# Attention tiles with 64 columns of their own for each half of 64 tokens (320 columns for 384), without block mask rows, and reciprocals spread as two 16-bit halves

## The chip, the cores and the metric

The kernel runs on one core of a Trainium2 chip. The metric is the time of the whole program on the device, in microseconds. Everything below is about that one core: its TensorE (PE; PEld is its weight load), VectorE (DVE), ScalarE (ACT), GpSimd (POOL), and SyncE (SP), whose queue issues most of the DMAs.

## The reference, cut to what matters

Two layers work on x of 8 sequences x 1024 tokens x 256. Each is an attention of 16 heads with 16 dimensions a head, and a feed-forward part; the change touches the attentions and the step that follows the first one.

```python
# layer 0: every query sees the keys at most 128 tokens away
out_of_window = abs(idx[:, None] - idx[None, :]) > 128
att = softmax(where(out_of_window, fmin, q @ k.T) / 16)
x = x + (att @ v) @ Wp.T + bp
# then a mixture of 8 experts, on layernorm(x)
# layer 1: blocks of 64 tokens; block 0 and the last block see all keys, a middle
# block n sees block 0, blocks n-1, n, n+1 and the last block (blocks 1 and -2 alike)
ctx = softmax(q @ k.T * 0.25 over those keys) @ v
x = x + ctx
# then a ternary linear layer, on x
```

## The kernel before, in words

`stage_attend` (lines 453 to 883) is built twice, as "a0" for layer 0 and "a1" for layer 1. Its unit of work is one sequence and one group of four heads: 32 units a layer. Tokens are cut in 8 tiles of 128. A list of jobs says which keys a tile of queries is multiplied with. In layer 0 (`window_jobs`) tile t takes the columns of tiles t-1, t and t+1: 384 columns, 256 for the first and the last tile, so 6 jobs of 384 and 2 of 256. In layer 1 (`block_jobs`) tile 0 holds the first and the last block and takes all 1024 columns in two jobs of 512; tiles 7 to 1 take tile 0 and their neighbourhood with half a tile on each side: 384 columns, 320 for tiles 7 and 1. That is 9 jobs. Blocks that only one half of a tile may see are taken out by four more rows in the contraction (`block_rows`, loaded by ACT's queue in `start`, lines 760 and 761), so that the product of -65504 and 32768 is added there.

Each job of each of the four heads is done twice on TensorE, both times by `product` (line 769, the matmul is line 775):

- `score_tile` makes scores with the queries' tile as the stationary operand, into a bank of the ring psc (3 banks). DVE's `maxima` takes the maximum of each row: in layer 0 with a mask added (line 687, a custom instruction followed by a read of its accumulator), in layer 1 with a plain reduction (line 692). POOL scales the maxima, TensorE turns them (line 809), ACT copies them (line 718), and SP's queue stores them as one more row of the operand (`rows_of_max`, line 582).
- `prob_tile` makes the same scores with the keys' tile as the stationary operand and the maximum subtracted, into a bank of pst (3 banks). ACT takes the exponential (line 740) into pr. In layer 0 POOL sets the corners outside of the window to zero (line 658). `with_v` multiplies by the values (line 836): 17 columns stationary for each of four heads at the tile positions 0, 32, 64 and 96, in 32-bit, which the compiler makes two passes of one matmul.

The contraction has 48 to 53 rows, so heads go in pairs, one on rows 0 to 63 of the array and one on rows 64 to 127. The order of the work is written out by hand in TensorE's `step`: for each job two blocks of (probabilities n, scores n of the unit after next, probabilities n+1, scores n+1), and behind each block half of the `with_v` of an earlier job (two jobs before in layer 0, one in layer 1). The first two units' scores are made alone, in `start`. In the last two units no scores are left to make.

SP's queue carries, for each unit: 12 loads of q and k (lines 564 and 565, `reload_qk`, after the last `prob_tile` of the unit before), 4 stores of maxima (line 582, `rows_of_max`), the load of the values (line 574), 4 stores of the output (line 598) and one of the sums (line 600), in that order.

`stage_combine` ("c0") divides the output of layer 0 by its sums and multiplies by Wp. `Shares` makes the reciprocals (`invert`, DVE line 905) and spreads a head's reciprocal over its 16 rows by a matmul with a 0/1 matrix (`over_rows`, line 912), in 32-bit: two passes of 512 columns for each of two halves e and each of 16 chunks c. DVE multiplies (line 1022), ACT and POOL split the product in two 16-bit halves (992, 1007), TensorE multiplies by Wp (lines 68 to 70, 24 matmuls of 256 columns a chunk), DVE adds (1029) and takes statistics (112).

## Time and profile before

| | |
|---|---|
| Median of 3 runs | 2443.06 us (2439.72 to 2443.52) |
| The profiled execution's own time | 2437.45 us |
| Its span from the first to the last instruction | 2435.7 us |
| Busy share of the span | PE 90%, DVE 76%, ACT 68%, POOL 44% |
| Attention of layer 0 | about 165 to 695 us |
| Combination | about 700 to 790 us |
| Attention of layer 1 | about 1671 to 2300 us |

In the rows below a group of instructions is named by its line, its engine and "out<-in" with the program's names for tiles, and by its shape: 48*128 48x384 is a matmul of 48 contracted rows, 128 stationary columns and 384 moving columns. A timeline row gives the start, the time from the first start to the last end, how many instructions it merges (x4), and in brackets how long the engine was idle before and what ended that. A matmul's length in the trace contains the latency of the array, so the distance from start to start says what it costs when many follow each other. SPq is SyncE's queue, each row the issue of a DMA.

### The profile page before, as it was taken

The page shows a single profiled execution, that of the slowest core. Times are in us where ns is not written, and L with a number is a line of the kernel's source. Part 1 is how long each engine was busy: PE and PEld are TensorE (multiplying, and loading weights), DVE is VectorE, ACT ScalarE, POOL GpSimd, SP SyncE. Part 2 cuts the span into 40 slices and gives each one's busy share as a digit, 9 for nine tenths or more (in the row PEclk, how much of TensorE's full clock was granted, in tenths as well). Part 3 has the DMA queues.
Part 4 walks back from the last instruction along what each step waited for, and adds up shares of the span by engine and source line. Part 5 has one row for each costly group of instructions (what it writes and reads, how often), then busy time and mean ns, then how long its engine had stood idle before and what let it go on. Part 6 is the DMA issues. An engine that isn't in the chain of part 4 may idle for free. (4 is left out here: it accounts for less than half of the span.)

```text
span 2435.7 us, 73430 instructions
## 1 busy us (share of the span) xinstructions
PE 2200.0 (90%) x25549; PEld 1344.8 (55%) x25549; DVE 1840.5 (76%) x5599; ACT 1661.7 (68%) x3892; POOL 1072.9 (44%) x1370
## 2 busy tenths in 40 slices
PE   7979999999969688879999995996999999999765
PEld 4643444444436576768888884563444444444354
DVE  5539999999829577755445444984999999999298
ACT  7955888889942555525445443893699999999644
POOL 3533666666654466646666664562000000000076
PEclk9987999999979899989999998997899999999888
DMA  6552333333232567646654344884232232322242
GB/s 231 199 183 72 91 91 92 92 90 92 67 89 77 138 189 187 163 129 125 144 127 106 92 92 118 270 274 149 63 80 74 78 79 78 79 75 68 65 152 96
DMA packets 363698, 289.65 MB, mean 119 GB/s; under 512 B 228401, under 2 KB 296753, under 8 KB 363345
## 3 DMA queue, kind: packets, MB, share of 16 engines
q1 hardware_dynamic: 349616, 248.24, 37.2%
q0 software_dynamic: 12960, 35.60, 4.5%
q8 instruction: 220, 3.60, 0.6%
q10 hardware_dynamic: 768, 1.12, 0.2%
q14 instruction: 134, 1.09, 0.1%
HBM read 133.53 MB, written 123.69 MB: 106 GB/s over the span
## 5 line engine op out<-in xcount | busy, mean ns | idle before, releaser
L740 ACT ACTIVATE a_pr<-a_pst 128x384 f32<-128x384 f32 (+3 forms) x2176 | 908.8, 486 | 117.0 <-PE a_pst L775 79.7
L775 PE MATMUL a_psc<-a_ke,a_qe 52*128 52x128 f16 (+5 forms) x3072 | 648.6, 291 | 32.7 <-DMA a_ke<-mrow 29.2
L692 DVE TENSOR_REDUCE a_mx<-a_psc 128x1 f32<-128x384 f32 (+2 forms) x1152 | 566.9, 564 | 18.9 <-PE a_psc L775 13.7
L775 PE MATMUL a_pst<-a_qe,a_ke 53*128 53x128 f16 (+5 forms) x3072 | 564.3, 281 | 2.7 <-ACT a_pr L740 0.4
L836 PE MATMUL a_po<-a_pr,a_ve 128*17 128x128 f32 (+3 forms) x10496 | 562.1, 302 | 2.0 <-ACT a_pr L740 1.2
L687 DVE CUSTOM_DVE_ANT_0 a_cut<-a_psc,row_mask 128x384 bf16<-128x384 f32 (+1 forms) x1024 | 472.7, 521 | 23.4 <-PE a_psc L775 11.5
L775 PEld LDWEIGHTS a_pst<-a_qe,a_ke 53*128 53x128 f16 (+1 forms) x3072 | 210.3, 94 | 330.1 <-ACT a_pr L740 187.5
L658 POOL TENSOR_SCALAR_AFFINE_SELECT a_pr<-a_pr 128x512 f32<-128x512 f32 x448 | 275.1, 634 | 163.2 <-ACT a_pr L740 163.2
L775 PEld LDWEIGHTS a_psc<-a_ke,a_qe 52*128 52x128 f16 (+1 forms) x3072 | 223.5, 94 | 143.7 <-DVE a_mx L692 44.5
L836 PEld LDWEIGHTS a_po<-a_pr,a_ve 128*17 128x17 f32 x10496 | 193.9, 96 | 191.2 <-issue 116.3
L638 POOL TENSOR_SCALAR a_mneg<-a_mx 128x32 f16<-128x32 f32 x64 | 18.4, 288 | 632.5 <-DVE a_mx L696 588.1
L1671 DVE SCALAR_TENSOR_TENSOR e_hid<-e_pgu,e_gate 128x256 f32<-128x256 f32 x213 | 90.5, 425 | 213.0 <-ACT e_gate L1615 211.9
L68 PE MATMUL e_pgu<-e_xt,uh 128*128 128x256 f16 x852 | 233.3, 274 | 8.1 <-DMA e_xt<-xs 8.1
L315 POOL TENSOR_TENSOR p_stg<-p_qk,p_stg 128x512 f16<-128x512 f32 x128 | 164.4, 1290 | 159.7 <-ACT p_qk L355 157.2
L70 PE MATMUL e_pgu<-e_xt,ul 128*128 128x256 f16 x852 | 233.3, 274 | 0.0
L69 PE MATMUL e_pgu<-e_xt,uh 128*128 128x256 f16 x852 | 233.3, 274 | 0.0
L1615 ACT ACTIVATE e_gate<-e_pgu 128x256 f32<-128x256 f32 x213 | 81.5, 383 | 210.3 <-PE e_pgu L70 210.3
L1590 POOL TENSOR_TENSOR e_hl<-e_hid,e_hh 128x256 f16<-128x256 f32 x213 | 140.9, 675 | 121.1 <-ACT e_hh L1619 119.3
L1216 POOL DMA_INDIRECT xs<-g_xrow,g_slot x128 | 134.5, 1051 | 92.4 <-DVE g_slot L1348 60.2
L1598 POOL DMA_INDIRECT y<-e_yst,e_dest x142 | 138.0, 972 | 39.8 <-issue 23.4
L68 PE MATMUL e_py<-dh,e_hh 128*128 x426 | 116.2, 273 | 2.4 <-POOL e_hl L1590 2.4
L70 PE MATMUL e_py<-dh,e_hl 128*128 x426 | 116.2, 273 | 0.0
(234 smaller groups left out, 4172.7 us busy)
## 6 DMA issues: line engine op xcount, KB each, us to landing
a_qe<-qx SPq DMA_DIRECT2D x378, 64.0 KB, 2.6
a_ke<-kx SPq DMA_DIRECT2D x378, 64.0 KB, 2.7
vx<-p_vst SPq DMA_DIRECT2D x32, 544.0 KB, 3.4
a_ve<-vx SPq DMA_DIRECT2D x64, 272.0 KB, 3.1
qx<-p_stg SPq DMA_DIRECT2D x64, 256.0 KB, 3.4
kx<-p_stg SPq DMA_DIRECT2D x64, 256.0 KB, 3.3
ox<-a_ost SPq DMA_DIRECT2D x256, 64.0 KB
x_res<-x SPq DMA_DIRECT2D x16, 512.0 KB, 8.9
```

The costliest lines, as they stand in the source:

```text
L68: pe.matmul(out, stat_hi(p), mov_hi(p), start=(a == 0), stop=False)
L69: pe.matmul(out, stat_hi(p), mov_lo(p), start=False, stop=False)
L70: last = pe.matmul(out, stat_lo(p), mov_hi(p), start=False, stop=(a == n - 1))
L315: pool.tensor_tensor(stg[:, b % 2, m, 1, cols], qk32[:, m, :], stg[:, b % 2, m, 0, cols], ALU.subtract).then_inc(qk_lo, 1)
L658: pool.affine_select(out=edge, in_=edge, compare_op=ALU.is_ge, fill=0.0, base=0, pattern=[[0, 4], [sign, width]], channel_multiplier=-sign)\
L687: dve.tensor_tensor_reduce(out=cut[:, n % 4, 0:width], in0=psc[(u * n_s + n) % RING][:, 0:width], in1=row_mask[:, at:at + width], scale=1. ...
L692: dve.tensor_reduce(out.unsqueeze(1), psc[(u * n_s + n) % RING][:, 0:width], AXX, ALU.max)\
L740: act.activation(pr[s % SLOTS][:, h // 2, h % 2, 0:width], pst[prob_slot(u, n) % RING][:, 0:width], ACT.Exp, scale=scale).then_inc(p_ready, 1)
L775: last = pe.matmul(out[:, col:col + count], stat, mov(tok, count), start=(k == 0), stop=(k == len(pieces) - 1), skip_group_check=True, til ...
L836: last = pe.matmul(po[h][32 * a:32 * a + VW, tok % CH:tok % CH + w], ve[g][:, t, a * VW:(a + 1) * VW], pr[s % SLOTS][:, a // 2, a % 2, col ...
L1590: pool.tensor_tensor(hl[:, j % 2, f, :], hid[:, f, :], hh[:, j % 2, f, :], ALU.subtract)\
L1598: pool.indirect_dma_start(y2[:, :], bass.IndirectOffsetOnAxis(ap=dest[:, g, t:t + 1], axis=0), yst[:, g, t, :], None).then_inc(scattered[g ...
```

## The change

- Layer 0: a middle tile t takes one piece of 256 columns that both halves of its 128 tokens share (from 64 tokens before the tile to 64 behind it), and an edge of 64 columns in which each half has tokens of its own: the 64 before the piece for the first half, the 64 behind it for the second. 320 columns for 384. The first and the last tile keep 256.
- Layer 1: tiles 7 to 1 take tile 0 and their own tile as one strided piece of 256, and an edge of 64 for each half: 320 columns for all. The two jobs of 512 stay.
- `product` issues everything by halves of 64 stationary columns, at column position 0 or 64 of the array: two edge matmuls of 64 columns where a job has edges, two matmuls of 256 (or 512) columns, and in layer 0's `prob_tile` two more of 64 columns, which add a corner mask (`corner16`) to the edge. A score tile is 4 matmuls, a probability tile 6 in layer 0 and 4 in layer 1, where it was 1 in layer 0, 2 or 1 in layer 1; tiles without edges are 2.
- `with_v` multiplies the edge columns twice, once for each half's destination, with values whose other half of 64 rows is zero (`vez`). They are loaded by two more DMAs a unit on SP's queue, and the zeros are set once by POOL.
- Layer 0's POOL masks keep their number and are 64 wide for 128 in middle tiles; the mask of `maxima` comes from a loaded table `corner`.
- The four mask rows and their loads go (16 DMAs of ACT's queue in layer 1). Layer 0 loads `corner` by one DMA on ACT's queue.
- `Shares` splits the reciprocals in two 16-bit halves, the high one by ACT and the low one by DVE, each once for 512 columns and twice in the stage, and spreads them by two 16-bit matmuls.

```diff
+    jobs = [(0, [(0, 2 * P, 0)], None, [(P, P, 1, 0)])]
+    for t in range(1, TB - 1):
+        lo = t * P - 64
+        jobs.append((t, [(lo, 2 * P, 0)], (lo - 64, lo + 2 * P, True, True), [(0, 64, 0, 64), (3 * 64, 64, 1, 0)]))
+    return jobs + [(TB - 1, [(N - 2 * P, 2 * P, 0)], None, [(0, P, 0, 0)])]
...
+        left, right = t > 1, t < TB - 1
+        edges = (t * P - 64 if left else t * P, t * P + P if right else t * P + 64, left, right)
+        jobs.append((t, [(0, P, 0), (t * P, P, P)], edges, []))
...
+                v = vx[bass.ds(b * N, N), g * 4 * VW:(g + 1) * 4 * VW].rearrange("(t p) w -> p t w", p=P)
+                sp.dma_start(ve[g][:, :, :], v).then_inc(v_loaded[g], 16)
+                for half in range(2):
+                    r = slice(64 * half, 64 * half + 64)
+                    sp.dma_start(vez[r, half, g, :, :], v[r, :, :]).then_inc(v_loaded[g], 16)
...
+                pool.memset(vez[64:P, 0, :, :, :], 0.0).then_inc(vez_set, 1)
+                pool.memset(vez[0:64, 1, :, :, :], 0.0).then_inc(vez_set, 1)
+                pool.wait_ge(vez_set, 2)
...
+            if jobs[s][2]:
+                a, b, left, right = jobs[s][2]
+                edges = [(1, a, 64, widths[s] - 64)] * left + [(2, b, 64, widths[s] - 64)] * right
...
-                    for col, width, which in jobs[s][2]:
+                    for col, width, which, base in jobs[s][3]:
...
-            def product(par, out, stat, mov, pieces, ready):
-
-                for k, (tok, count, col) in enumerate(pieces):
-                    last = pe.matmul(out[:, col:col + count], stat, mov(tok, count), start=(k == 0),
-                                     stop=(k == len(pieces) - 1), skip_group_check=True, tile_position=(64 * par, 0))
+            def product(par, out, t, stat, mov, job, cornered, ready):
+
+
+                _t, pieces, edges, _m = job
+                end = sum(p[1] for p in pieces)
+                halves = [slice(64 * half, 64 * half + 64) for half in range(2)]
+                for half in range(2) if edges else ():
+                    pe.matmul(out[halves[half], end:end + 64], stat[:, t * P + 64 * half:t * P + 64 * half + 64],
+                              mov[:, edges[half]:edges[half] + 64], start=True, stop=False, skip_group_check=True,
+                              tile_position=(64 * par, 64 * half))
+                for half in range(2) if edges and cornered else ():
+                    r = slice(64 * par, 64 * par + 64)
+                    pe.matmul(out[halves[half], end:end + 64], corner16[r, 0:64], corner16[r, 64 + 64 * half:128 + 64 * half],
+                              start=False, stop=False, skip_group_check=True, tile_position=(64 * par, 64 * half))
+                for half in range(2):
+                    if len(pieces) == 2:
+                        to = out[halves[half], 0:end].rearrange("p (t c) -> p t c", c=P)
+                        of = mov.rearrange("k (t c) -> k t c", c=P)[:, 0:t + 1:t, :]
+                    else:
+                        to, of = out[halves[half], 0:end], mov[:, pieces[0][0]:pieces[0][0] + end]
+                    last = pe.matmul(to, stat[:, t * P + 64 * half:t * P + 64 * half + 64], of, start=not edges, stop=True,
+                                     skip_group_check=True, tile_position=(64 * par, 64 * half))
                 last.then_inc(ready, 1)
...
+                            cols = slice(a * VW, (a + 1) * VW)
+                            stat = vez[:, kind - 1, g, t, cols] if kind else ve[g][:, t, cols]
                             last = pe.matmul(po[h][32 * a:32 * a + VW, tok % CH:tok % CH + w],
-                                             ve[g][:, t, a * VW:(a + 1) * VW], pr[s % SLOTS][:, a // 2, a % 2, col:col + w],
+                                             stat, pr[s % SLOTS][:, a // 2, a % 2, col:col + w],
...
+    def high(self, act, half):
+        cols = slice(half * CH, half * CH + CH)
+        act.wait_ge(self.ready, half + 1)
+        act.activation(self.rec_hi[:, cols], self.rec[:, cols], ACT.Copy, scale=SHS).then_inc(self.high_done, 1)
+
+    def low(self, dve, half):
+        cols = slice(half * CH, half * CH + CH)
+        dve.wait_ge(self.high_done, half + 1)
+        dve.scalar_tensor_tensor(out=self.rec_lo[:, cols], in0=self.rec[:, cols], scalar=SHS, in1=self.rec_hi[:, cols],
+                                 op0=ALU.mult, op1=ALU.subtract).then_inc(self.low_done, 1)
+
     def over_rows(self, pe, out, c, e):
         if c < 2:
             pe.wait_ge(self.set, 3)
-            pe.wait_ge(self.ready, c + 1)
+            pe.wait_ge(self.low_done, c + 1)
         at = ((c // 2) * EC + e) * P
-        return pe.matmul(out, self.spread[:, at:at + P], self.rec[:, (c % 2) * CH:(c % 2) * CH + CH],
-                         start=True, stop=True)
+        cols = slice((c % 2) * CH, (c % 2) * CH + CH)
+        pe.matmul(out, self.spread[:, at:at + P], self.rec_hi[:, cols], start=True, stop=False)
+        return pe.matmul(out, self.spread[:, at:at + P], self.rec_lo[:, cols], start=False, stop=True)
```

## Rows read from the trace of the kernel before

**Rows 1.** Busy time by engine in 60 us of each attention (windows)
```profile
300.00:360.00 60.00, 59.72 (x829) 24.74 (x827) 58.58 (x255) 54.05 (x139) 40.00 (x68) 1.00 0.36 92
...
1800.00:1860.00 60.00, 60.00 (x1069) 29.87 (x1069) 59.38 (x125) 55.54 (x131) 0.86 (x3) 1.00 0.27 75
```

**Rows 2.** ACT's copy of the turned maxima, once a unit (timeline, both attentions)
```profile
409.08 0.25 ACT L718 ACTIVATE a_mt<-a_pst 32x128 f16<-32x128 f16 x1
...
424.27 0.26 ACT L718 ACTIVATE a_mt<-a_pst 32x128 f16<-32x128 f16 x1
...
1996.65 0.27 ACT L718 ACTIVATE a_mt<-a_pst 32x128 f16<-32x128 f16 x1
...
2014.69 0.27 ACT L718 ACTIVATE a_mt<-a_pst 32x128 f16<-32x128 f16 x1
```

**Rows 3.** DVE's maxima, three of layer 0 and a whole unit of layer 1 (timeline)
```profile
403.29 0.55 DVE L687 CUSTOM_DVE_ANT_0 a_cut<-a_psc,row_mask 128x384 bf16<-128x384 f32 x1
...
403.76 0.42 DVE L687 CUSTOM_DVE_ANT_0 a_cut<-a_psc,row_mask 128x256 bf16<-128x256 f32 x1
...
404.11 0.42 DVE L687 CUSTOM_DVE_ANT_0 a_cut<-a_psc,row_mask 128x256 bf16<-128x256 f32 x1
...
1682.98 17.35 DVE L692 TENSOR_REDUCE a_mx<-a_psc 128x1 f32<-128x512 f32 x36 [10.10 <-PE a_psc L775]
```

**Rows 4.** PE, blocks of products and of with_v, one after the other (timeline, both layers)
```profile
400.17 0.33 PE L775 MATMUL a_pst<-a_qe,a_ke 49*128 49x384 f16 x1
...
400.61 0.41 PE L836 MATMUL a_po<-a_pr,a_ve 128*17 128x128 f32 x8
400.95 0.33 PE L775 MATMUL a_pst<-a_qe,a_ke 49*128 49x384 f16 x1
...
401.65 0.63 PE L836 MATMUL a_po<-a_pr,a_ve 128*17 128x128 f32 x16
...
2001.12 0.23 PE L775 MATMUL a_pst<-a_qe,a_ke 53*128 53x128 f16 x1
...
2001.18 0.27 PE L775 MATMUL a_pst<-a_qe,a_ke 53*128 53x256 f16 x1
...
2001.56 0.41 PE L836 MATMUL a_po<-a_pr,a_ve 128*17 128x128 f32 x8
```

**Rows 5.** PE, 16-column products with 128 stationary columns, cold and warm clock (timeline)
```profile
2307.20 0.60 PE L1807 MATMUL t_ps<-ident,t_sums 16*128 16x16 f32 x4 [8.65 <-DMA t_ot<-ox]
2307.73 1.97 PE L1814 MATMUL t_pt<-ident,t_ot 128*128 128x128 f32 x8
...
2350.31 0.41 PE L1807 MATMUL t_ps<-ident,t_sums 16*128 16x16 f32 x4
2350.66 1.09 PE L1814 MATMUL t_pt<-ident,t_ot 128*128 128x128 f32 x8
```

**Rows 6.** SP's queue, one unit of layer 0 (timeline); its longest wait, 240 to 660 us
```profile
404.58 0.61 SPq L564 DMA_DIRECT2D a_qe<-qx  x1
...
413.27 2.78 SPq L582 DMA_DIRECT2D a_qe<-a_mt  x4
416.09 0.44 SPq L574 DMA_DIRECT2D a_ve<-vx  x1
416.64 3.25 SPq L598 DMA_DIRECT2D ox<-a_ost  x4
...
420.53 0.62 SPq L564 DMA_DIRECT2D a_qe<-qx  x1
...
SPq L564 <- PE a_pst L775: 20.0, 21, 1.9
```

**Rows 7.** The combination, one chunk on PE; DVE's waits, 728 to 780 us
```profile
725.71 1.88 PE L912 MATMUL c_pb<-c_rec,c_spread 128*128 128x512 f32 x4
...
730.05 1.88 PE L912 MATMUL c_pb<-c_rec,c_spread 128*128 128x512 f32 x4
...
DVE x_res L1029 <- PE c_py L70: 5.1, 12, 0.4
```

**Rows 8.** Layer 1's start: ACT's queue and PE's first product (timeline)
```profile
1676.04 0.71 ACTq L760 DMA_DIRECT2D a_qe<-brows  x1
...
1682.36 1.01 PE L775 MATMUL a_psc<-a_ke,a_qe 52*128 52x512 f16 x3 [15.69 <-DMA a_ke<-mrow]
```

More of the change, by code:

```diff
@@ L462, in stage_attend @@
     masked = row_mask is not None
-    KS = TK + (0 if const_rows is None else 4)
+    KS = TK
     KR = KS + 1
@@ L504, in stage_attend @@
         N_STORE = 5
-        N_CUT = sum(len(m) for _, _, m in jobs)
-        cuts_to = [sum(len(m) for _, _, m in jobs[:s + 1]) for s in range(nj)]
+        N_CUT = sum(len(job[3]) for job in jobs)
+        cuts_to = [sum(len(job[3]) for job in jobs[:s + 1]) for s in range(nj)]
+        widths = [sum(p[1] for p in job[1]) + (64 if job[2] else 0) for job in jobs]
         block = ctx.enter_context(nc.Block())
@@ L678, in maxima @@
                     j, par, i = n // 4, 1 - n % 2, n // 2 % 2
-                    t, pieces, mask_list = jobs[j]
-                    width = sum(p[1] for p in pieces)
+                    t, _p, edges, mask_list = jobs[j]
+                    width = widths[j]
                     out = mx2[:, u % 2, par, i, at_zero.index(j)] if len(at_zero) == 2 and t == 0 else mx[g % 2][:, par, i, t]
@@ L683, in maxima @@
                     if mask_list:
-                        at = 0 if t > 0 else P
+                        mask = corner[:, 0:width] if edges else row_mask[:, 0:width] if t else row_mask[:, P:P + width]
                         after(dve, s_read, u * n_s + n - 3)
@@ L731, in step @@
                 for s in range(nj):
-                    t, pieces, _m = jobs[s]
-                    width = sum(p[1] for p in pieces)
+                    width = widths[s]
                     after(act, p_used, u * nj + s - SLOTS + 1)
@@ L795, in prob_tile @@
                 s, i = n // 4, n // 2 % 2
-                t, pieces, _m = jobs[s]
                 if n == 0:
+                    if masked and unit(g, b) == 0:
+                        pe.wait_ge(c_rounded, 1)
                     pe.wait_ge(m_loaded[g], b * 64 + 64)
@@ L800, in prob_tile @@
                 free_to(pe, k - RING)
-                product(par, pst[k % RING], ke[g][rows(par, KR), i, t * P:(t + 1) * P],
-                        lambda tok, count: qe[g][rows(par, KR), i, tok:tok + count], pieces, t_ready)
+                product(par, pst[k % RING], jobs[s][0], ke[g][rows(par, KR), i, :], qe[g][rows(par, KR), i, :],
+                        jobs[s], masked, t_ready)
             def turn(g, b):
@@ L992, in high @@
                     act.activation(ah[:, c % AR, e, :], att[:, c % 2, e, :], ACT.Copy).then_inc(a_hi, 1)
+            for half in range(2):
+                shares.high(act, half)
             act.wait_ge(s_w, 16)
@@ L2034, in build @@
 def build(nc, x, l0_wqkv, l0_bqk, l0_bv, l0_wp, l0_bp, gate_w, up_w, down_w, l1_wqkv, l1_bqk, l1_bv,
[L2035 removed]
+          tern_w, tern_alpha, tern_bias, masks, out):
     qx = nc.dram_tensor("qx", [2, 2 * HG, DH, 2, T], F16, kind="Internal").ap()
```

118 lines of the change are left out of this document (61 added, 57 removed).

## The prediction

> **What bounds the kernel now.** I read the windows first, to see which engines are full in each attention, then the period of a unit, then what each engine needs of it if nothing holds it up. In both attentions PE and DVE are busy over 97% of 60 us, ACT about 90% [rows 1]. A full PE proves little, since its lengths hold latency, so I count from start to start. A unit lasts 424.27 - 409.08 = 15.19 us in layer 0 and 18.04 in layer 1 [rows 2]; some 30 of each 32 run at that pace.
>
> DVE: in layer 0 a maximum over 384 columns costs 0.47 and one over 256 costs 0.35 [rows 3], so 24 x 0.47 + 8 x 0.35 = 14.1 us of 15.19. In layer 1, while nothing else runs, the 36 of a unit take 17.35 [rows 3], about 17.5 with the join, of 18.04. DVE is the bound in layer 1, and in layer 0's wide jobs.
>
> PE: a block of four products of 384 columns takes 0.44 from its start to `with_v` (400.17 to 400.61), in layer 1 the same (2001.12 to 2001.56). `with_v` with 8 matmuls of 128 columns takes 0.34 and 8 more cost 0.22 (0.63 less 0.41) [rows 4]: 0.12 a block and 0.22 for 128 columns. 256 columns stream in 0.11 less 384's 0.16, so a block of 256 is 0.33. Layer 0: 12 x 0.44 + 4 x 0.33 = 6.6, `with_v` 22 x 0.22 + 16 x 0.12 = 6.8 (2816 columns a unit), 0.15 for the turn: 13.5 of 15.19. Layer 1: 14 x 0.44 + 4 x 0.55 = 8.4, with_v 28 x 0.22 + 18 x 0.12 = 8.3, turn: 16.8 of 18.04. So PE stands 1 to 2 us behind DVE: it is next in line.
>
> SP's queue: its loop, from one unit's first load to the next one's, took 15.95 in the unit shown, with 8.69 for the 12 loads, 2.82 for the maxima, 0.55 for the values and 3.89 for the stores; it waits for PE 20.0 us in the 27.6 units of that stretch, 0.7 a unit [rows 6]. So it needs about 14.4 of layer 0's 15.19. In layer 1 it has over 3 us to spare.
>
> **The change, part by part.**
>
> DVE and ACT lose 64 columns in 24 tiles of layer 0 and in 20 of layer 1. At 0.12 for 128 columns [rows 3] that is 0.06 each: DVE needs 24 x 0.41 + 8 x 0.35 = 12.6 in layer 0 and 17.5 - 1.2 = 16.3 in layer 1. ACT, at most 54.05/60 of the period now, loses about as much. POOL is 67% busy in layer 0 and its masks get narrower. None of them bounds then.
>
> `with_v`: a middle job had 384 columns, and has 256 + 2 x 64 = 384: PE gains nothing there. It issues more pieces (240 matmuls a unit for 144 in layer 0); I take 0.1 a unit for them.
>
> Products: this decides. A block had 4 matmuls; it has 20 in layer 0's middle (6 + 4, twice) and 16 in layer 1. No row shows 64 x 64 tiles, so I bound a block from both sides. Low: all four quadrants of the array run beside each other and the longest chain counts, 64 + 64 + 256 in layer 0, as long as before (0.44), and 320 in layer 1 (0.44 less 2 x 0.03 = 0.38). That `with_v` runs its four column positions side by side, from separate data (8 matmuls, 0.34 in all), speaks for that [rows 4]. High: weight loads follow each other. Four 128-column loads with 16-column products take 0.35 warm and 0.53 cold [rows 5], so 64 columns cost at most 0.044 warm: 20 x 0.044 + 0.1 = 0.98, and 16 x 0.044 + 0.1 = 0.80. Between: matmuls start in the order of issue, so the second head's long matmul waits until the first one's has started, at 0.06 + 0.04 us, and the next pair needs its rows: 0.2 for one pair, 0.3 to the last long start, 0.11 streaming, 0.1 to change over: 0.50. Layer 1, without corners, 0.45. I take these, being nearest to the rows of `with_v`.
>
> The Trainium skill ("TensorE: Matmul & The Clock Gate", LDWEIGHTS) prices a load at columns / 1.2 ns, and its "TensorEngine Tiling (Array Packing)", Restrictions, says that column tiling turns the fast weight load off; both speak against this change. By them 64 columns take 53 ns, longer than a 64-column product streams, and a block would be 0.63 and 0.52. The warm rows allow no more than 0.35/4 = 0.088 for 128 columns, where the page has 0.107; the cold ones fit it. No run shows the fast load being off.
>
> PE's sum then: layer 0, 12 x 0.50 + 4 x 0.35 + 6.9 + 0.15 = 14.5; layer 1, 14 x 0.45 + 4 x 0.57 + 8.4 + 0.15 = 17.1.
>
> SP: two more DMAs a unit behind the load of the values, each like that one 0.44 to 0.55; bounds 0.35 and 0.7 (a load of q). 14.4 + 0.95 = 15.35. Queued behind them are the stores, then the next loads and the maxima that PE's next unit waits for. So layer 0 goes from DVE's pace to SP's: 15.3 for 15.19, +4 us in 30 units. In layer 1 the 0.95 has cover. DMA traffic grows by 0.27 MB a unit on a share of 0.36: nothing, at most 0.1 a unit.
>
> Layer 1: 17.1 on PE plus what it still waits, 0.4 to 0.5: 17.6 for 18.04, -13 us in 30 units.
>
> Starts: layer 0's two units of maxima alone save 48 x 0.06 = 3 and lose 0.7 to the load of the table; layer 1's save 40 x 0.06 = 2.4, and PE's first product waits for a row issued behind four mask loads, 0.7 + 0.5 each pair [rows 8]: 2 us earlier. Tails 1 each. Together -8. POOL's two memsets lie beside DVE's first unit.
>
> Combination: the four 32-bit passes of a chunk take 4 x 0.43 = 1.72, four 16-bit ones 0.86. A chunk takes 730.05 - 725.71 = 4.34, all PE; DVE waits 5.1/12 = 0.42 of it, and about 0.1 more inside its adds [rows 7]. So DVE bounds next: -0.5 x 14 = -7, at most -12 without DVE's bound. The split adds a step of ACT and one of DVE (1.5 us) twice ahead of the first spreads, which are 0.85 shorter each in the cold clock, and the third saves its 1.9: -2 net, and could be +2.
>
> Sum: +4 - 13 - 8 - 9 = -26, against the profiled execution's 2437.45: 2411.5. The median of the runs is 5.6 higher, 2443.06, so I forecast 2417.
>
> **The rivals.**
>
> *Loads seen, side by side.* If a 64-column load costs 0.044 and each quadrant hides its own, blocks become 0.58 and 0.49: PE 15.4 and 17.7 a unit, periods 15.6 and 18.0. +12 + 0 - 17 = -5: 2438. For it: the warm bound; against: that bound holds the products too. By the skill's 53 ns it would be 0.63 and 0.52, 16.0 and 18.1 on PE: some 2460.
>
> *The halves don't overlap (slower).* If the two halves on the same rows take turns at loads or data, a pair costs 6 and 4 loads in a row, a block about 0.80 in layer 0 and 0.65 in layer 1. PE becomes the bound at 12 x 0.80 + 1.6 + 7.05 = 18.3 and 14 x 0.65 + 2.3 + 8.55 = 19.9: +3.1 x 30 + 1.9 x 30 = +150, less 17: 2576. It turns the whole to a loss from 0.035 us more a block than I take (26 us over 26 blocks x 30 units). For it: 64-row and 64-column positions mixed are nowhere in the trace. Against: `with_v`.
>
> *Issue.* A unit has 512 (layer 0) and 528 matmuls, each with its load, for 208 and 312. The most in a long stretch is 1069 in 60 us, 0.056 each [rows 1], which is demand and no limit. If PE takes 0.04 each, 20.5 and 21.1 us a unit: +250, 2670.
>
> *SP is cheaper.* If the new DMAs cost 0.3, layer 0 goes at PE's 14.8: -12 instead of +4: 2401.
>
> **How the numbers follow.** Forecast 0.46, SP cheaper 0.08, loads seen 0.16 (half of it within 0.2%), halves in turn 0.22, issue 0.08. 0.2% (5 us) is what a measurement of this kernel can tell from no change. Faster 0.56, same 0.10, slower 0.34. The range leaves out issue and the upper half of the turns, and the gains below 2395: 2395 to 2530. The likeliest case's own range is 2400 to 2432.
>
> **What would show it.** Right: turns 17.6 apart in layer 1 and 15.3 in layer 0, SP's queue without waits for PE there, DVE's maxima 0.41 apart when free and idle between; blocks of products 0.50 and 0.45; chunks of the combination 3.85 apart with DVE full. Wrong: blocks over 0.54 and 0.49, PE's weight loads idle on "issue" inside a block, or a unit of layer 0 far from SP's sum.

## The result, and the profile after

**2529.55 us** median of 4 runs (2522.13 to 2540.54), 2442.85 for the kernel before beside them: a ratio of 1.0361, 95% interval 1.0321 to 1.0401. The change makes the kernel slower by some 87 us. The profiled execution took 2527.63 us, 90.2 more than the one of before. By the first and last matmuls of each stage they lie so: attention of layer 0 +61.4 us, combination -9.5, experts and projection +4.8, attention of layer 1 +30.0, the rest +3.3.

The page's parts 1 to 3 of the changed kernel; the last row is the queue that brings instructions (packets, MB, share), and for it the row of before follows:

```profile
span 2525.9 us, 106328 instructions
...
PE 2213.6 (88%) x41933; PEld 1570.0 (62%) x41933; DVE 1791.9 (71%) x5601; ACT 1613.4 (64%) x3895; POOL 996.4 (39%) x1374
...
PEclk9977999999997899979999998996899999999977
...
q8 instruction: 348, 5.70, 1.0%
```
```profile
q8 instruction: 220, 3.60, 0.6%
```

PE has 41933 matmuls for 25549 and is busy for a smaller share of the span; so is DVE. In the attentions neither of them is full any more. The windows (the second one 50 us later than in [rows 1]), where [rows 1] had PE and DVE at 58.5 to 60 of 60 us (columns: PE, PEld, DVE, ACT, POOL busy, clock, DMA share, GB/s):

```profile
300.00:360.00 60.00, 54.04 (x1749) 35.94 (x1743) 48.54 (x224) 44.31 (x123) 26.73 (x61) 1.00 0.42 101
1850.00:1910.00 60.00, 56.56 (x1595) 34.45 (x1587) 52.12 (x112) 48.69 (x119) 0.87 (x3) 0.94 0.35 85
```

The clock does not explain it: over 241 to 652 us it was 1.00 of 2.4 GHz, over 1819 to 2249 us 0.99, and 1.00 before in both.

ACT's copy once a unit, the 4th and the 31st of each layer (timeline), for the 15.19 and 18.04 of [rows 2]:

```profile
241.79 0.25 ACT L747 ACTIVATE a_mt<-a_pst 32x128 f16<-32x128 f16 x1
...
710.08 0.25 ACT L747 ACTIVATE a_mt<-a_pst 32x128 f16<-32x128 f16 x1
...
1818.09 0.27 ACT L747 ACTIVATE a_mt<-a_pst 32x128 f16<-32x128 f16 x1
...
2337.22 0.27 ACT L747 ACTIVATE a_mt<-a_pst 32x128 f16<-32x128 f16 x1
```

27 units each: (710.08 - 241.79) / 27 = 17.34 us a unit and 19.23, where the same count gives 15.24 and 18.04 before. All periods below are means worked out so.

What PE does in layer 1 (timeline), in place of [rows 4], and the two ends of one block of products in layer 0:

```profile
1944.86 0.22 PE L808 MATMUL a_pst<-a_qe,a_ke 49*64 49x64 f16 x2
1944.87 0.22 PE L808 MATMUL a_psc<-a_ke,a_qe 48*64 48x64 f16 x2
1944.91 0.28 PE L821 MATMUL a_pst<-a_qe,a_ke 49*64 49x256 f16 x2
...
1945.27 0.41 PE L881 MATMUL a_po<-a_pr,a_ve 128*17 128x128 f32 x8
1945.50 0.29 PE L881 MATMUL a_po<-a_pr,a_vez 128*17 128x64 f32 x8
1945.73 0.22 PE L808 MATMUL a_pst<-a_qe,a_ke 49*64 49x64 f16 x2
...
1946.37 0.28 PE L881 MATMUL a_po<-a_pr,a_vez 128*17 128x64 f32 x3
1948.28 0.30 PE L881 MATMUL a_po<-a_pr,a_vez 128*17 128x64 f32 x5 [1.63 <-issue]
```
```profile
415.68 0.22 PE L808 MATMUL a_pst<-a_qe,a_ke 49*64 49x64 f16 x2
...
416.14 0.41 PE L881 MATMUL a_po<-a_pr,a_ve 128*17 128x128 f32 x8
```

The block of products costs 1945.27 - 1944.86 = 0.41, less than I had forecast (0.45), and half a job (a block of products and its share of `with_v`) 0.87 in all; a block of layer 0 costs 416.14 - 415.68 = 0.46. Over all 27 units the median of layer 1's blocks with edges is 0.42. In layer 0 a quarter of them take 0.45 or less and the median is 0.53, waits included.

Then, in the middle of eight equal matmuls, PE stands for 1.63 us and waits for nothing that the profile shows.

I counted PE's records (matmuls, weight loads, semaphore and register instructions) in order of their starts. In the 27 units of both layers there are 88 stops of over 0.6 us, and all 88 lie at the same place in each run of 256 records; the kernel before has no stop of over 0.6 us in its 27 units. The trace has 89064 records of PE, and 5.70 MB in 348 packets is 64 bytes for each record and 16384 bytes a packet: 256 instructions.

The packets also tell what a stop waits for. Each took about 1.1 us. The 135 stops of over 0.3 us at that place vary in length from 0.3 to 1.9 us, and every one of them ended 1.2 to 1.8 us after such a packet had ended, half of them within 1.4. **PE runs out of instructions.** The steps from record to record at that place, the ordinary 0.06 included, sum to 2.39 us a unit in layer 0 and 1.76 in layer 1; before, no such place has more than 0.12.

How long 256 instructions take, stop excluded, and what the stop adds (counted at each such place in the changed kernel's 27 units, us; 34 of the 227 rounds fall in ranges that are not listed):

| 256 instructions ran in | number | mean stop behind them | sum |
|---|---|---|---|
| under 3.00, layer 0 | 5 | 1.11 | 4.04 |
| 3.00 to 3.25, layer 0 | 18 | 0.99 | 4.15 |
| 3.25 to 3.50, layer 0 | 23 | 0.72 | 4.09 |
| 3.75 to 4.25, layer 0 | 49 | 0.39 | 4.37 |
| 3.25 to 3.50, layer 1 | 45 | 0.76 | 4.15 |
| 3.50 to 3.75, layer 1 | 20 | 0.39 | 4.00 |
| over 4.50, layer 1 | 33 | 0.03 | 5.33 |

So where it asks for them fastest, PE gets 256 instructions in some 4.0 to 4.2 us on average, though single ones came through in 3.3. The stops don't end sharply at 4.0: in layer 0, 49 of the 111 rounds ran in 3.75 to 4.25 us and still had 0.39 behind them; why the supply took longer there is open. The parts of such a round in layer 0, as medians: 1.65 us from that place to the start of the next packet, 1.1 for the packet, and 1.4 until PE goes on. In the kernel before, the first part is 0.9 us, and each packet had started over 6 us before layer 0 came to that place. Half a job of layer 1 is 32 matmuls, 32 loads and 2 others in 0.87 us: 256 in 3.4.

The Trainium skill ("Runtime: NRT & Kernel Launch", Instruction fetch mechanics) describes this fetch, "refilled in 16 KiB blocks (256 instructions)", and calls the cost of a boundary "mostly hidden". The block's size agrees with the trace; that it is hidden does not: the stops of over 0.3 us at that place sum to 58.0 us in the 27 units of layer 0 alone.

SP's queue, one unit of layer 0 (timeline), for [rows 6]; its longest wait, 260 to 640 us:

```profile
409.63 0.59 SPq L585 DMA_DIRECT2D a_qe<-qx  x1
...
411.53 1.30 SPq L586 DMA_DIRECT2D a_ke<-kx  x1
...
415.41 1.36 SPq L585 DMA_DIRECT2D a_qe<-qx  x1
...
420.59 0.45 SPq L596 DMA_DIRECT2D a_ve<-vx  x1
421.08 1.33 SPq L599 DMA_DIRECT2D a_vez<-vx  x2
...
426.17 0.59 SPq L585 DMA_DIRECT2D a_qe<-qx  x1
```
```profile
SPq L585 <- PE a_pst L821: 10.2, 21, 1.1
```

The two new loads take 0.67 each in this unit and 0.81 on average from 260 to 640 us, not 0.44 to 0.55, and issues that usually take 0.59 take 1.3 more often: 58 of 526 took over 0.9 us between 260 and 640 us, 27 of 550 before. With 10.2 us of waits in 21.9 units, SP's queue needs 16.9 of the 17.34; before, it needed 14.5. So layer 0 has two new bounds close to each other.

The combination's chunk is now 787.99 - 784.51 = 3.48 (4.34 in [rows 7]), and DVE's first unit of maxima in layer 1 takes 16.04 (17.35 in [rows 3]). Shown are the chunk, a window of the combination, and DVE's maxima: two of layer 0 over 320 columns, 0.41 apart, and layer 1's first unit:

```profile
784.51 0.38 PE L972 MATMUL c_pb<-c_rec_hi,c_spread 128*128 128x512 f16 x1
...
787.99 0.38 PE L972 MATMUL c_pb<-c_rec_hi,c_spread 128*128 128x512 f16 x1
```
```profile
785.00:795.00 10.00, 10.00 (x84) 8.00 (x83) 9.90 (x23) 2.46 (x4) 4.54 (x4) 1.00 0.33 107
```
```profile
411.54 0.49 DVE L714 CUSTOM_DVE_ANT_0 a_cut<-a_psc,a_corner 128x320 bf16<-128x320 f32 x1
...
411.95 0.49 DVE L714 CUSTOM_DVE_ANT_0 a_cut<-a_psc,a_corner 128x320 bf16<-128x320 f32 x1
...
1739.95 16.04 DVE L719 TENSOR_REDUCE a_mx<-a_psc 128x1 f32<-128x512 f32 x36 [7.72 <-PE a_psc L821]
```

### The profile page after: what moved, and what is told of

It reads as the page before. It is cut to its first block and busy times, and to the rows that moved or that the text cites. A ratio compares the mean times of both kernels' runs of the same rounds, so it can differ in the third digit from the quotient of the medians.

```text
span 2525.9 us, 106328 instructions
## 1 busy us (share of the span) xinstructions
PE 2213.6 (88%) x41933; PEld 1570.0 (62%) x41933; DVE 1791.9 (71%) x5601; ACT 1613.4 (64%) x3895; POOL 996.4 (39%) x1374
## 3 DMA queue, kind: packets, MB, share of 16 engines
q14 instruction: 135, 1.11, 0.1%
## 5 line engine op out<-in xcount | busy, mean ns | idle before, releaser
L768 ACT ACTIVATE a_pr<-a_pst 128x320 f32<-128x320 f32 (+2 forms) x2176 | 849.7, 449 | 246.9 <-PE a_pst L821 233.1
L821 PE MATMUL a_psc<-a_ke,a_qe 48*64 48x256 f16 (+1 forms) x4352 | 568.9, 301 | 37.4 <-DMA a_ke<-mrow 28.1
L719 DVE TENSOR_REDUCE a_mx<-a_psc 128x1 f32<-128x320 f32 (+1 forms) x1152 | 544.7, 529 | 69.9 <-PE a_psc L821 63.6
L821 PE MATMUL a_pst<-a_qe,a_ke 49*64 49x256 f16 (+1 forms) x4352 | 521.7, 291 | 11.3 <-issue 9.4
L881 PE MATMUL a_po<-a_pr,a_ve 128*17 128x128 f32 (+2 forms) x9984 | 500.6, 278 | 18.2 <-issue 13.1
L714 DVE CUSTOM_DVE_ANT_0 a_cut<-a_psc,a_corner 128x320 bf16<-128x320 f32 x768 | 343.0, 489 | 74.8 <-PE a_psc L821 60.1
L808 PE MATMUL a_psc<-a_ke,a_qe 48*64 48x64 f16 x3328 | 332.9, 212 | 9.0 <-issue 5.8
L808 PE MATMUL a_pst<-a_qe,a_ke 49*64 49x64 f16 x3328 | 319.3, 205 | 9.9 <-issue 4.4
L662 POOL TENSOR_SCALAR a_mneg<-a_mx 128x32 f16<-128x32 f32 x64 | 18.5, 289 | 642.2 <-DVE a_mx L723 607.9
L821 PEld LDWEIGHTS a_pst<-a_qe,a_ke 49*64 49x64 f16 x4352 | 229.6, 107 | 57.9 <-issue 23.4
L881 PE MATMUL a_po<-a_pr,a_vez 128*17 128x64 f32 x6144 | 243.7, 222 | 24.5 <-issue 24.1
L808 PEld LDWEIGHTS a_pst<-a_qe,a_ke 49*64 49x64 f16 x3328 | 163.4, 106 | 138.5 <-ACT a_pr L768 42.4
```

The lines of the kernel that those rows point to most:

```text
L714: dve.tensor_tensor_reduce(out=cut[:, n % 4, 0:width], in0=psc[(u * n_s + n) % RING][:, 0:width], in1=mask, scale=1.0, scalar=-3.0e38, op0 ...
L719: dve.tensor_reduce(out.unsqueeze(1), psc[(u * n_s + n) % RING][:, 0:width], AXX, ALU.max)\
L768: act.activation(pr[s % SLOTS][:, h // 2, h % 2, 0:width], pst[prob_slot(u, n) % RING][:, 0:width], ACT.Exp, scale=scale).then_inc(p_ready, 1)
L808: pe.matmul(out[halves[half], end:end + 64], stat[:, t * P + 64 * half:t * P + 64 * half + 64], mov[:, edges[half]:edges[half] + 64], star ...
L821: last = pe.matmul(to, stat[:, t * P + 64 * half:t * P + 64 * half + 64], of, start=not edges, stop=True, skip_group_check=True, tile_posi ...
L881: last = pe.matmul(po[h][32 * a:32 * a + VW, tok % CH:tok % CH + w], stat, pr[s % SLOTS][:, a // 2, a % 2, col:col + w], start=(h not in o ...
```

## The experiments

Three theories. A: instruction supply. B: 64-wide tiles or their weight loads cost more in the array. C: SP's queue, with the two loads of edge values. The table has each run against the kernel before on its own chip, the periods, PE's instructions a unit and the stops at each 256th, summed over a unit (layer 0 / layer 1). e1, g3, g2 and e4 edit the kernel before, the others the changed kernel. Four leave work out: e2 and e5 use the first sequence's edge values for all sequences, g4 also leaves out layer 0's corner masks, and k1 also `with_v` of layer 1's edge columns:

| Run | median us | ratio, 95% | period | instructions | stops |
|---|---|---|---|---|---|
| before | | | 15.24 / 18.04 | 454 / 666 | 0.08 / 0.12 |
| the change | 2529.55 | 1.0361 (1.0321-1.0401) | 17.34 / 19.23 | 1047 / 1098 | 2.39 / 1.76 |
| e1, before, matmuls cut | 2546.25 | 1.0426 (1.0402-1.0450) | 16.35 / 20.54 | 999 / 1306 | 1.02 / 2.70 |
| g3, before, halves alone | 2460.00 | 1.0073 (1.0054-1.0092) | 15.53 / 18.35 | 582 / 922 | 0.11 / 0.11 |
| g2, before, edge loads alone | 2466.80 | 1.0094 (1.0075-1.0113) | 16.26 / 18.04 | 454 / 666 | 0.16 / 0.12 |
| e2, edge values once | 2514.11 | 1.0301 (1.0274-1.0328) | 16.91 / 19.12 | 1047 / 1098 | 1.90 / 1.75 |
| e3, with_v cut less | 2511.11 | 1.0279 (1.0245-1.0314) | 17.08 / 19.37 | 966 / 1034 | 0.99 / 1.72 |
| e5, e2 and e3 | 2470.77 | 1.0118 (1.0100-1.0136) | 15.99 / 18.71 | 966 / 1034 | 0.77 / 1.33 |
| g4, e5 without corners | 2457.56 | 1.0053 (1.0032-1.0074) | 15.78 / 18.96 | 870 / 1034 | 0.45 / 1.35 |
| k1, e5, fewer edges in 1 | 2412.24 | 0.9875 (0.9834-0.9915) | 16.00 / 16.75 | 966 / 842 | 0.79 / 0.15 |
| e4, shares alone | 2436.06 | 0.9966 (0.9951-0.9981) | 15.24 / 18.04 | 454 / 666 | 0.08 / 0.12 |
| f1, edge values by GpSimd | 2625.55 | 1.0737 (1.0705-1.0768) | 20.49 / 19.56 | 1047 / 1099 | 0.26 / 1.73 |
| g1, edges first | 2753.59 | 1.1289 (1.1254-1.1324) | 21.07 / 20.79 | 922 / 958 | 0.13 / 0.22 |
| f2, long product whole | 3933.17 | 1.6095 (1.6066-1.6123) | 37.66 / 43.30 | 918 / 954 | 0.20 / 0.38 |

**e1: more instructions without any 64-wide tile.**

```diff
 # product: pieces of over 192 columns in two; with_v:
-halves = [(tok, w // 2, col), (tok + w // 2, w - w // 2, col + w // 2)] if w > 3 * 64 else [(tok, w, col)]
-pieces += halves
+pieces += [(tok + at, 64, col + at) for at in range(0, w, 64)]
```

> The kernel before, with the same columns streamed by the same 128-wide tiles, no 64-wide tile anywhere and no change to SP's queue; only the matmuls are cut into shorter ones (with_v in pieces of 64 columns, products of over 192 columns in two halves), so that TensorE gets about 998 instructions a unit in layer 0 (454 before, 1047 in the changed kernel) and 1306 in layer 1 (666, 1098). Theory A (instruction supply: TensorE stops at each 256th instruction, once it takes less than 4.24 to 4.5 us for 256): a unit goes at instructions / 256 x 4.24 to 4.48, so 16.5 us in layer 0 (15.2 before) and 21.6 to 22.9 in layer 1 (18.0): +40 and +105 to +145, 2443 + 165 = about 2610 in all (2560 to 2635), with gaps on 'issue' at each 256th instruction. Theory B (64-wide tiles or their weight loads cost more in the array) and theory C (SP's two loads of the edge values hold the unit up): nothing here, 2440 to 2455.

+102 us by the medians, where B and C expected nothing, with the stops of A at the same place (73 of the 74 stops over 0.6 us in its 27 units):

```profile
2008.03 0.41 PE L842 MATMUL a_po<-a_pr,a_ve 128*17 128x64 f32 x14
...
2008.84 0.40 PE L842 MATMUL a_po<-a_pr,a_ve 128*17 128x64 f32 x10 [0.39 <-issue]
```
```profile
q8 instruction: 368, 6.03, 1.0%
```

Supply alone does this, then: the stops are 1.02 and 2.70 us a unit, where the periods grew by 1.11 and 2.50. The size was overrated in layer 1: I had multiplied by 4.24 to 4.48 us per 256, which holds waits for others too; here they took 4.03. This run has before's SP queue, and still 58 of its issues in that stretch took over 0.9 us (27 before), and g2, below, has 31 with the two loads alone: the slow issues come with the change of PE's instruction stream, not with the new loads.

**g3: the halves without the edges.**

```diff
+for half in range(2):
+    r = slice(64 * half, 64 * half + 64)
     for k, (tok, count, col) in enumerate(pieces):
-        last = pe.matmul(out[:, col:col + count], stat, mov(tok, count), ..., tile_position=(64 * par, 0))
+        last = pe.matmul(out[r, col:col + count], stat[:, r], mov(tok, count), ..., tile_position=(64 * par, 64 * half))
```

> The kernel before with each product in two matmuls of 64 stationary columns, the two halves of 64 tokens over the same columns; nothing else changes. 582 TensorE instructions a unit in layer 0 (454) and about 922 in layer 1 (666). Theory (64-wide halves run beside each other, instructions are in time): 15.2 to 15.3 us a unit in layer 0, 18.0 to 18.6 in layer 1 (3.6 blocks of 256 a unit, some of them dense): 2443 (2440 to 2462). Rival (64-wide tiles on the same rows take turns, or their weight loads show: a block +0.2 us and more): TensorE's sum grows by 3 to 5 us a unit, 2550 and more.

0.3 us a unit in either layer, nothing like 3 to 5: the halves run beside each other, and *The halves don't overlap* falls. What is left of B is those 0.3 us, 16 us in all: the weight loads of 64 columns have longer records than those of 128 (105 ns for 94), and most of that is hidden. The short edge products are not in this run; the changed kernel's own blocks, 0.41 and 0.46, speak for them. In layer 1 this run has 922 instructions a unit, but its 256 take 3.98 us at the fastest, and it hardly stops (0.11).

**g2: the loads alone.**

```diff
+for half in range(2):
+    r = slice(64 * half, 64 * half + 64)
+    sp.dma_start(vez[r, half, g, :, :], v[r, :, :]).then_inc(v_loaded[g], 16)
```

> The kernel before with the two loads of edge values a unit added to SP's queue, where nothing reads them; TensorE waits for them as in the change. SP's queue as bound: 14.5 us + 1.5 for the two + 0.2 around them + up to 0.7 in the other DMAs = 16.2 to 16.9 us a unit in layer 0 (15.24), layer 1 unchanged at 18.04: 2443 + 30 to 50 = 2485 (2470 to 2495). By the price of my prediction (0.95 for both) 15.4 a unit: 2450.

+1.02 us a unit in layer 0, none in layer 1: at the low end of what was expected and above my prediction's 0.1 to 0.2. This is from the profiled execution, the slowest of the four (2474.50, with a granted clock of 0.94 in layer 0); the median, 2466.80, is below the expected 2470 to 2495 and makes it some 0.7. SP waits 8.1 us for PE in 23.4 units here, so it needs 15.9: 14.5 + 1.4 for the two loads. In the changed kernel it needs 16.9; the last 1.0 is what is left over, and the slow issues fit it: in e1 an issue takes 0.66 us on average for 0.61 before, which is 1.1 in the 22 of a unit.

**e2 and e3: one bound removed at a time; e5: both.**

```diff
 # e2
-for half in range(2):
+for half in range(2) if b == 0 else ():
     sp.dma_start(vez[r, half, g, :, :], ...)
 # e3
-w = min(count, CH - tok % CH, P if count > 3 * 64 else count)
+w = min(count, CH - tok % CH, count if jobs[s][2] else widths[s] // 2)
```

> The changed kernel with the halves' own values of the edges loaded for the first sequence only, so that SP's queue has the DMAs of before again; the later sequences compute with the first one's values there (that part of the computation is changed). Theory A (instruction supply): nothing, the period stays at 17.3 us in layer 0 and 19.2 in layer 1, 2520 to 2530. Theory C (SP's queue and the traffic of these loads): the period goes to 15.3 and 17.6, about -110 us: 2420. Theory B (64-wide tiles cost more in the array): nothing.

> The changed kernel, where the matmuls of with_v over the shared keys are no longer cut at 128 columns but as long as a job and a chunk allow: 96 TensorE instructions fewer a unit in layer 0 (951 for 1047) and 64 fewer in layer 1 (1034 for 1098); columns, 64-wide tiles and SP's queue stay. Theory A (instruction supply): 951/256 x 4.24 = 15.8 us a unit in layer 0 (17.3) and 1034/256 x 4.48 = 18.1 in layer 1 (19.2): -48 and -35, about 2445 (2435 to 2475). Theories B (64-wide tiles) and C (SP's loads): at most a few us, 2515 to 2530.

> The changed kernel with both edits that each gave little alone: edge values loaded for the first sequence only (that part of the computation is changed) and with_v cut as seldom as may be. If layer 0 has two bounds side by side (SP's queue 17.1, instruction supply 16.9), both go: 15.5 to 16.1 us a unit there, layer 1 stays at 19.3: 2511 - 36 = 2475 (2465 to 2485). If the two small gains of 0.43 and 0.26 us a unit only add up: 2498.

Each alone gives 0.43 and 0.26 us a unit in layer 0, both together 1.35, and 2470.77 for an expected 2475: two bounds side by side, each hiding what the other's removal is worth. My expectation of e3 alone missed that. It missed in layer 1 too: no gain there, though 64 instructions a unit are gone. In the trace they came out of the two 512-wide jobs alone; a middle job's shared pieces were 128 wide already, and its half job still has 66 instructions in 0.87 us. What counts is how dense the instructions are where PE runs, not their number over a unit.

**g4: layer 0 without corners.**

```diff
-for half in range(2) if edges and cornered else ():
+for half in ():
```

> The kernel with edge values loaded once and with_v cut as seldom as may be (2471), without the 96 corner matmuls a unit of layer 0 (the masks of the edges' triangles are left out of the probabilities there): 774 TensorE instructions a unit in layer 0 for 966, layer 1 as it was. Instruction supply: the stalls at each 256th instruction go (0.77 us a unit), what is left is SP's queue at 15.5: 15.5 for 15.99 a unit, 2471 - 15 = 2456 (2450 to 2462). If the instructions are no matter in layer 0 now: 2466 to 2471. Layer 1 the same 18.7 in either case.

The text counts wrongly: it is 48 matmuls, 96 instructions a unit. It came out at -13 us by the medians, though only 0.2 us a unit shows in layer 0 in the profiled execution, which itself lay 15.5 above the median (the four others are at 2451 to 2461); it bears A out in direction, no more. The stops went from 0.77 to 0.45.

**k1: layer 1's middle jobs thinned out.**

```diff
-if (n < v_split(s)) == (part == 0):
+if (n < v_split(s)) == (part == 0) and (masked or not kind):
```

> The kernel with edge values loaded once and with_v cut as seldom as may be (2471), where layer 1 leaves out with_v of the edge columns (their part of the output is missing; layer 0 is as it was). It takes 192 TensorE instructions a unit out of layer 1's middle jobs (1034 to 842), their matmuls too. Instruction supply: 256 instructions of a middle job then take about as long as their fetch, the stalls go almost all, and VectorE (16.3 by my sum) sets the pace: 16.6 to 17.2 us a unit for 18.7 to 19.4, 2471 - 55 = 2415 (2400 to 2430). If something else of the change holds layer 1 (64-wide tiles, masks, waits between VectorE and ScalarE): 18 us a unit and more, 2450 and more. Layer 0 stays at 16.0.

2412.24 for an expected 2415, as A had it. Its copies once a unit (timeline, the 4th and the 31st of layer 1) and a window:

```profile
1776.23 0.27 ACT L747 ACTIVATE a_mt<-a_pst 32x128 f16<-32x128 f16 x1
...
2228.40 0.27 ACT L747 ACTIVATE a_mt<-a_pst 32x128 f16<-32x128 f16 x1
```
```profile
2000.00:2060.00 60.00, 59.71 (x1411) 28.94 (x1403) 58.55 (x132) 56.20 (x139) 1.15 (x4) 1.00 0.34 85
```

16.75 us a unit, the stops gone (0.15), DVE full again at 58.55 of 60: this is what the narrower tiles would be worth to DVE. The run also takes array time away, so it doesn't say alone that supply was the cause; with the table of stops it does fit.

**e4: the other half of the change.** `Shares` and `stage_combine` as in the diff, both attentions as before.

> The kernel before with the 16-bit halves of the reciprocals alone; both attentions stay as before. The combination falls from 93.5 us to about 84 as in the changed kernel: -9 us, 2434. A rival: part of the gain lies beside something else in the end, -4 or less.

-8.3 us. It is the version that beats both kernels with nothing left out; k1 is faster still, but leaves work out.

**f1: the edge values made by GpSimd.**

```diff
-sp.dma_start(vez[r, half, g, :, :], v[r, :, :]).then_inc(v_loaded[g], 16)
+pool.tensor_scalar(vez[:, half, g, :, :], ve[g][:, :, :], own[:, half:half + 1], None, ALU.mult)
```

> The changed kernel, its computation whole, with the halves' values of the edges made by GpSimd from the loaded values (two multiplications by 1 or 0 a unit) instead of two loads on SP's queue. If the runs so far are read rightly, the two loads cost SP 1.5 us a unit of their own and about 0.7 in stalls of the other DMAs, and SP's queue (17.1 us) and the instruction supply (16.9 us) stand side by side in layer 0: the period goes from 17.3 to 16.9 there and stays at 19.1 to 19.2 in layer 1, as with the edge values loaded once: 2514 (2505 to 2522). If GpSimd's copies get in the way of its masks or of VectorE: 2525 or more.

2625.55 for an expected 2514: slower by 3.2 us a unit in layer 0. The groups of GpSimd, 300 to 360 us:

```profile
L693 POOL TENSOR_SCALAR_AFFINE_SELECT a_pr<-a_pr 128x256 f32<-128x256 f32 (+1 forms) x43 | 18.1, 446 | 27.4 <-ACT a_pr L782 27.4
L667 POOL TENSOR_SCALAR a_vez<-a_ve,a_own 128x544 f32<-128x544 f32 x6 | 9.8, 1645 | 0.0
```

1.65 us each, 3.3 a unit, in front of the cuts of the next unit's first job: `with_v` now waits for GpSimd, 7.3 us in these 60, that is 2.5 a unit. The granted clock was 0.81 here, so a part of the loss may be the clock's. An engine at 45% of its time is no free one if its queue has work that others wait for.

**f2, f3, g1: fewer instructions by whole long products.**

```diff
 # f2 (f3: with f1 and e3 besides)
-for half in range(2):
-    last = pe.matmul(to, stat[:, t * P + 64 * half:t * P + 64 * half + 64], of, ..., tile_position=(64 * par, 64 * half))
+last = pe.matmul(to, stat[:, t * P:(t + 1) * P], of, ..., tile_position=(64 * par, 0))
 # g1: the same, but a block's edges all come ahead of its four long products
```

> The changed kernel, with the long product of each tile in one matmul of 128 stationary columns again and only the edges in two 64-wide ones: 919 TensorE instructions a unit in layer 0 (1047) and 954 in layer 1 (1098), and a layer 1 block of products has 24 for 32, so the densest stretches thin out, which cutting with_v less did not do. Instruction supply: layer 1 goes from 19.2 to 18.0 (17.6 to 18.4), layer 0 from 17.3 to SP's 17.0 only: 2527 - 36 - 9 = 2482 (2465 to 2495). If it is the count over a unit alone that matters, layer 1 is at 954/256 x 4.48 = 16.7, that is at its next bound 17.6: 2470. If 64-wide tiles in mixed company cost a change of mode, slower than 2527.

> The changed kernel, its computation whole, with the three edits together: GpSimd makes the edge values, the long products are whole, with_v is cut as seldom as may be; some 838 TensorE instructions a unit in layer 0 and 890 in layer 1. Instruction supply and SP's queue both gone as bounds: 15.3 to 15.6 us a unit in layer 0 and 17.6 in layer 1, the combination as in the changed kernel: 2443 + 5 - 13 - 17 = 2418 (2410 to 2440), the forecast of the change itself. If something else of the change costs time, above 2450.

> The changed kernel with long products whole (128 stationary columns), as in the run that took 3933, but in each block of four products all 64-wide edges are issued first and the four long ones after them. There the array seemed to run empty at each change between a 64-wide and a 128-wide tile (a product each 0.52 us at a granted clock near 0.55, 8 changes of form a block), here 2 changes lie in a block and one on the way to with_v. Theory (a change costs 0.06 to 0.12 us): about 1.6 to 3 us a unit over the changed kernel's own sum of TensorE, minus the stalls for instructions: 17.5 to 18.5 us in layer 0, 19.5 to 21 in layer 1, 2560 (2500 to 2700). If it is whole long products beside 64-wide ones as such, or the cold clock that feeds itself, that costs: above 3000.

The costliest miss: 3933 us for an expected 2482, and f3 3926.48 (ratio 1.6076, 1.6047 to 1.6105). A block of f2 in layer 1 (timeline), and a window of it:

```profile
2800.85 0.26 PE L808 MATMUL a_pst<-a_qe,a_ke 49*64 49x64 f16 x2
2801.04 0.39 PE L820 MATMUL a_pst<-a_qe,a_ke 49*128 49x256 f16 x1
2801.36 0.26 PE L808 MATMUL a_psc<-a_ke,a_qe 48*64 48x64 f16 x2
2801.55 0.39 PE L820 MATMUL a_psc<-a_ke,a_qe 48*128 48x256 f16 x1
```
```profile
300.00:360.00 60.00, 60.00 (x720) 30.22 (x720) 23.56 (x101) 21.86 (x54) 11.85 (x27) 0.53 0.13 31
```
```profile
PEclk9855555555555578999999895556555555555568
```

A product every 0.51 us, one after the other, even on the two halves of the rows that used to run beside each other; PE is "busy" for 60 of 60 us with 720 matmuls. The granted clock (last row, the page's 40 slices) was near its upper level of 2.4 GHz until the first attention ran such blocks, then lay near the lower one, 1.2 GHz, and rose again between the attentions, where PE has full-width matmuls. g1, with the same matmuls grouped, has (timeline, layer 1, clock 1.00)

```profile
2103.73 0.22 PE L810 MATMUL a_pst<-a_qe,a_ke 49*64 49x64 f16 x2
...
2104.00 0.28 PE L826 MATMUL a_pst<-a_qe,a_ke 49*128 49x256 f16 x1
...
2104.32 0.41 PE L885 MATMUL a_po<-a_pr,a_ve 128*17 128x128 f32 x8
```

0.59 a block for the change's 0.41, with one change of form more: so a change of form costs some 0.2 us or a little less there, more than the 0.06 to 0.12 I had read out of f2. In all it came at 2753.59, above the range of 2500 to 2700. Its layer 1 came at 20.79, as expected; layer 0, at a clock of 0.59, at 21.07, above the 18.5 expected; why the clock stays low in the one layer and not in the other is open. The Trainium skill ("TensorEngine Tiling (Array Packing)", Tiling Modes) says that changing the tiling mode "drains the TensorE"; both runs agree. The changed kernel changes form too, between products and `with_v`, as the kernel before did.

**h1, h2, i1, i2: instructions that use no array.** Ahead of each matmul of `with_v` in the kernel before:

```diff
+pe.sem_inc(counted[again % 2], 1)   # h1: 8 in layer 0, 4 in layer 1; h2: half
+pe.wait_ge(again, least)            # i1: 17 and 9 long met waits, two to an instruction; i2: half
```

> The kernel before with TensorE instructions added that use no array and no data: increments of two semaphores that nobody waits for, eight ahead of each matmul of with_v in layer 0 and four in layer 1. Some 1029 instructions a unit in layer 0 (454) and 1032 in layer 1 (666), as many as the changed kernel's 1047 and 1098, with the matmuls, weight loads and DMAs of before. Instruction supply: stalls at each 256th instruction, 4.0 blocks x 4.1 to 4.25 us = 16.5 to 17.1 us a unit in layer 0 (15.24), in layer 1 18.1 to 19 (18.04), and SP's issues over 0.9 us near 58 in the 380 us of layer 0 where there were 27: 2443 + 55 = 2498 (2480 to 2540). Rival (matmuls and weight loads are what costs): 2443 to 2450. If an increment costs TensorE's queue time of its own, 0.02 us each, it is slower still, but without the stalls at each 256th.

> The same with half as many: 742 instructions a unit in layer 0 (2.9 blocks of 256 in 15.2 us) and 850 in layer 1 (3.3 in 18.0). Instruction supply: each block has 5.2 and 5.4 us, over the 4.1 that a fetch takes, so few stalls or none: 2443 to 2455. Rival (each added instruction costs time of its own): half of what the other run loses.

> The kernel before with TensorE instructions added that use no array and no data: waits on semaphores that have long passed their value, eight instructions ahead of each matmul of with_v in layer 0 and four in layer 1 (the compiler puts two waits into one instruction). 1030 instructions a unit in layer 0 (454) and about 1049 in layer 1 (666), with the matmuls, weight loads and DMAs of before. Instruction supply: stalls at each 256th instruction, 4.0 blocks x 4.1 to 4.25 us = 16.5 to 17.1 us a unit in layer 0 (15.24), 18.1 to 19 in layer 1 (18.04), SP's issues over 0.9 us near 58 in the 380 us of layer 0 for 27: 2443 + 55 = 2498 (2480 to 2540). Rival (matmuls and weight loads cost, not instructions): 2443 to 2450. If a met wait costs queue time of its own as the increments did: far above 2540, and the other run half as far.

> The same with half as many: 742 instructions a unit in layer 0 (2.9 blocks of 256, 5.2 us for each) and 865 in layer 1 (3.4 blocks, 5.3 us for each). Instruction supply, which takes 4.1 us a block: few stalls or none, 2443 to 2455. Waits with a price of their own: half of what the other run loses.

6360.76, 4044.21, 5168.37 and 3547.18 us. The instruction queue had 118, 59, 120 and 61 packets more than before, so an increment costs (6360.76 - 2439.53) / (118 x 256) = 0.130 us, 0.106 in the half dose, and an instruction of met waits 0.089 and 0.071. The granted clock is in these prices too: 0.68, 0.92, 0.80 and 0.96 over the span, for 0.95 before. PE never comes near the rate at which supply would show (17.3 us for 256 in layer 0 of i1), and it stops at each matmul instead: these four say nothing on A. Whether instructions without matmuls are enough for the stops was not shown; that would need a kind that costs well under 4.1 / 256 = 0.016 us.

## Why the prediction was wrong

The forecast was 2417 and faster; it is 2529.55 and slower. The range's upper end (2530) just holds it, but by a mechanism it was not stretched for.

- **Supply, the step that failed.** In *Issue* I called 1069 matmuls in 60 us "demand and no limit", priced a limit per matmul and gave it 0.08; everywhere else a unit's instructions, from 454 to 1047, cost "0.1 a unit". They cost 2.39 and 1.76 us a unit in stops. The limit is not one of each matmul but of 256 instructions, in 4.0 to 4.2 us. The row gave the means: 1069 matmuls and as many loads in 60 us are 256 instructions in 7.2 us [rows 1], and the fastest 256 in the attentions of before took 5.6; my own half job of layer 1 (0.45 and some 0.45 for `with_v`) asks for 66 in 0.9, 256 in 3.5, a density that the trace of before shows nowhere.
- **SP's queue.** I took 0.95 for the two loads and "15.35" for the unit. They cost 1.4 (g2), and another 1.0 goes, as far as e1 shows it, to the slow issues that come with PE's new stream: 16.9. Even with supply free, layer 0 would have lost some 0.7 to 1 us a unit (g2).
- **TensorE's sum was right, near enough.** Without the stops a unit is 17.34 - 2.39 = 14.95 (14.5 forecast, and other waits are in the 14.95) and 19.23 - 1.76 = 17.47 (17.6). The blocks, the step on which I spent most of the argument, came at 0.45 and 0.41 where nothing held them up, for 0.50 and 0.45. That leaves no room for *Loads seen* (0.58 and 0.49), and *The halves don't overlap* fell with g3. Slower weight loads show in their records, but cost at most g3's 0.3 us a unit. Layer 0 has 505 matmuls a unit, not 512.
- **DVE was right**: 0.41 for 320 columns, 16.04 for the first unit, 16.75 a unit once it is the bound (k1).
- **The combination's total was right by luck**: -9.5 us in the change and -8.3 alone, for -9, out of two terms that were both off. A chunk fell by 0.86 to 3.48, all that PE saves, and not by 0.5: DVE, at 9.90 of 10 us in the new chunks, needs no more than 3.45 a chunk. Before, the same work was busy for 8.9 of 10 us, 3.9 a chunk, so more of that than the 0.1 I took was waits. That is -12 over 14 chunks, so the start and the rest lost some 2.5 where I had -2.
- By stage the forecast was +4 and -13 in the attentions' units, with -8 at starts and tails. It is +57 and +32 in 27 units each. The +4.8 between them and +3.3 at the end are not explained.

## What to carry to other kernels

Count an engine's instructions, loads and semaphores included, in the densest stretch and not over the whole, and compare with what the trace shows it was fed: here some 4.1 us for 256 on TensorE. Splitting matmuls into more and shorter ones to save columns pays only while the supply keeps up. Where two bounds lie close together, removing one gives little (0.43 and 0.26 us of 1.35), and only a run without both shows what either is worth.
